# The diagonal mask of attention scores moved from TensorE to VectorE, and the reciprocals of the row sums from VectorE to GpSimd

## The reference, cut to what matters

```python
dots = jnp.einsum('bhid,bhjd->bhij', q, k) * jnp.exp(temperature)
eye = jnp.eye(n, dtype=bool)
dots = jnp.where(eye, NEG_MAX, dots)
attn = jax.nn.softmax(dots, axis=-1)
out = jnp.einsum('bhij,bhjd->bhid', attn, v)
```

## Time and profile before

| | before |
|---|---|
| median of 3 runs | 501.92 us (501.88 to 503.92) |
| profiled execution | 501.19 us |
| its span, first to last instruction | 499.4 us |
| TensorE clock granted, mean | 0.999 of full speed |
| busy: TensorE matmul | 478.2 us, 96% |
| busy: VectorE | 398.6 us, 80% |
| busy: ScalarE | 363.9 us, 73% |
| busy: GpSimd | 231.1 us, 46% |

### The profile page before, as it was taken

The page is one execution under the profiler, slowest core; times in us unless marked ns, Lnnn a source line. Parts: engine busy times, 40 slices in busy tenths (PEclk is TensorE's granted clock), DMA queues, the critical chain, the costliest instruction groups (busy, mean ns, idle before and its releaser), DMA issues.

```text
span 499.4 us, 11296 instructions
## 1 busy us (share of the span) xinstructions
PE 478.2 (96%) x3936; PEld 398.5 (80%) x3936; DVE 398.6 (80%) x738; ACT 363.9 (73%) x688; POOL 231.1 (46%) x226
## 2 busy tenths in 40 slices
PE   2999999999999999999999999999999999999887
PEld 2955788888888888888788888888888888888775
DVE  5469999878887887788887888788878899989455
ACT  1258788888788778877888688878887788683543
POOL 1112586667346734663246735663566345541000
PEclk9999999999999999999999999999999999999999
DMA  6500019432943295361612592349234933000002
GB/s 234 211 1 0 2 44 214 92 86 58 195 95 84 48 194 108 85 137 43 127 62 66 109 194 52 81 99 197 53 84 90 194 66 84 1 1 3 3 13 76
DMA packets 29483, 44.78 MB, mean 90 GB/s; under 512 B 3200, under 2 KB 21120, under 8 KB 29184
## 3 DMA queue, kind: packets, MB, share of 16 engines
q1 hardware_dynamic: 28864, 44.21, 37.6%
q10 hardware_dynamic: 576, 0.00, 0.1%
HBM read 6.46 MB, written 1.05 MB: 15 GB/s over the span
## 4 chain that ended last, share of the span: by engine, by line
PE 90%; DVE 5%; DMA 2%; ACT 2%; issue 1%; SPq 0%; POOL 0%; DVEq 0%; ACTq 0%
PE ps L686 24%; PE ps L670 22%; PE ps L654 11%; PE ps L655 11%; PE ps L596 5%; PE ps L729 3%; PE ps L591 2%; PE ps L658 2%; DMA arena<-in_wqkv_rows 2%; PE ps L877 2%; PE ps L860 2%; PE ps L891 1%; DVE pt_lo L1351 1%; DVE neg_max L1363 1%; PE ps L566 1%; PE ps L842 1%
## 5 line engine op out<-in xcount | busy, mean ns | idle before, releaser
L431 POOL TENSOR_SCALAR probs<-probs,inv_sum 128x1024 f32<-128x1024 f32 x128 | 144.8, 1131 | 184.3 <-DVE inv_sum L1357 181.6
L1363 DVE TENSOR_REDUCE neg_max<-ps 128x1 f32<-128x1024 f32 x128 | 156.6, 1223 | 63.9 <-PE ps L658 63.8
L1026 ACT ACTIVATE pt_hi<-ps 128x512 fp32r<-128x512 f32 x256 | 139.2, 595 | 39.7 <-PE ps L670 39.6
L1351 DVE TENSOR_TENSOR pt_lo<-ps,pt_hi 128x512 fp32r<-128x512 f32 x256 | 162.3, 676 | 1.5 <-ACT pt_hi L1026 1.5
L686 PE MATMUL ps<-pt_hi,v_slot 128*128 128x256 f32 x512 | 150.2, 326 | 0.0
L1046 ACT ACTIVATE probs<-ps,neg_max 128x1024 f32<-128x1024 f32 x128 | 142.5, 1113 | 1.5 <-DVE neg_max L1363 0.7
L670 PE MATMUL ps<-ident,probs 128*128 128x128 f32 x1024 | 133.8, 274 | 0.7 <-DVE v_all L1271 0.6
L686 PE MATMUL ps<-pt_lo,v_slot 128*128 128x256 f32 x512 | 127.7, 281 | 0.0
L670 PEld LDWEIGHTS ps<-ident,probs 128*128 128x128 f32 x1024 | 110.1, 141 | 1.3 <-DVE v_all L1271 0.7
L686 PEld LDWEIGHTS ps<-pt_hi,v_slot 128*128 128x128 f32 x512 | 96.6, 189 | 9.7 <-issue 9.7
L686 PEld LDWEIGHTS ps<-pt_lo,v_slot 128*128 128x128 f32 x512 | 96.8, 189 | 8.8 <-issue 8.8
(11 more groups left out here) (141 smaller groups left out, 404.8 us busy)
## 6 DMA issues: line engine op xcount, KB each, us to landing
q_st<-arena SPq DMA_DIRECT2D x28, 256.0 KB, 3.7
k_hi<-arena SPq DMA_DIRECT2D x28, 256.0 KB, 5.1
k_lo<-arena SPq DMA_DIRECT2D x28, 256.0 KB, 5.3
v_slot<-v_all SPq DMA_DIRECT2D x14, 512.0 KB, 3.9
arena<-arena SPq DMA_DIRECT2D x28, 256.0 KB, 5.4
f_sb<-in_f SPq DMA_DIRECT2D x2, 1024.0 KB, 10.7
x<-in_tok SPq DMA_DIRECT2D x2, 512.0 KB, 7.8
w_slot<-in_w_pairs SPq DMA_DIRECT2D x8, 128.0 KB, 2.1
```

The lines of the kernel that those rows point to most:

```text
L431: pool.tensor_scalar(probs[:, t % 4, :], probs[:, t % 4, :], inv_sum[:, t % 4:t % 4 + 1], 1.0, ALU.mult, ALU.mult).then_inc(norm_done, 1)
L1026: act.activation(dst, ps[:, transposes_bank(t, a, drain), :].rearrange("p (j c) -> p j c", c=P), ACT.Copy).then_inc(hi_done, 1)
L1351: dve.tensor_tensor(pt_lo[at], ps[:, transposes_bank(t, a, drain), :].rearrange("p (j c) -> p j c", c=P), pt_hi[at].bitcast(F32), ALU.subt ...
L1363: dve.tensor_reduce(neg_max[:, t % 4:t % 4 + 1], ps[:, SCORES + 2 * (t % 2):SCORES + 2 * (t % 2) + 2, :].rearrange("p a c -> p (a c)"), AX ...
```

## The change: what it does

In all head pairs but the first, TensorE's list loses the mask matmul, and the last score matmul counts `scores_ready`. VectorE gets a new function, `mask`: it waits for the scores, adds `neg_block` (a 128x128 f32 tile with -3e38 on its diagonal) in place to the diagonal block in PSUM, and counts `masked`. The maximum then waits for `masked`. In the first pair the mask stays on TensorE.

In all pairs the reciprocal leaves VectorE. GpSimd waits for the exponential (`exp_done`), raises the row sum to the power -1 into `inv_sum`, counts `recip_done`, waits for that, and normalises as before. Set-up on GpSimd gets three more instructions, so `N_CONST` goes from 12 to 15.

```diff
         def wait_apart(engine, semaphore, value):
...
+            const(pool.memset(neg_block[:, :], 0.0))
...
+            const(pool.memset(powers[:, 3 * NT:3 * NT + 1], -1.0))
...
-            for m, fill in ((ident, 1.0), (ident_b, 1.0), (neg_diag, NEG)):
+            for m, fill in ((ident, 1.0), (ident_b, 1.0), (neg_diag, NEG), (neg_block, NEG)):
...
                     for t in range(SPH):
                         split_qk(pair, k, t)
+                        wait_apart(pool, exp_done, pair.step0 + k * SPH + t + 1)
+                        pool.tensor_tensor(inv_sum[:, t % 4:t % 4 + 1], row_sum[:, t % 4:t % 4 + 1],
+                                           powers[:, 3 * NT:3 * NT + 1], ALU.pow).then_inc(recip_done, 1)
                         wait_apart(pool, recip_done, pair.step0 + k * SPH + t + 1)
...
                 own = t // 4
+                by_pe = pair.i == 0
                 for c in (1 - own, own):
...
-                    pe.matmul(bank, q, k_lo[:, k, half], start=False, stop=c != own)
-
-                bank = ps[:, SCORES + 2 * (t % 2) + own, :]
-                pe.matmul(bank[:, (t % 4) * P:(t % 4 + 1) * P], neg_diag[:, :], ident_b[:, :],
-                          start=False, stop=True).then_inc(scores_ready, 1)
+                    ins = pe.matmul(bank, q, k_lo[:, k, half], start=False, stop=c != own or not by_pe)
+
+                if by_pe:
+                    bank = ps[:, SCORES + 2 * (t % 2) + own, :]
+                    ins = pe.matmul(bank[:, (t % 4) * P:(t % 4 + 1) * P], neg_diag[:, :], ident_b[:, :],
+                                    start=False, stop=True)
+                ins.then_inc(scores_ready, 1)
...
-            def reciprocals(pair, k, t):
+            def mask(pair, k, t):
+
                 n = pair.step0 + k * SPH + t
-                dve.wait_ge(exp_done, n)
-                dve.reciprocal(inv_sum[:, (t - 1) % 4:(t - 1) % 4 + 1],
-                               row_sum[:, (t - 1) % 4:(t - 1) % 4 + 1]).then_inc(recip_done, 1)
+                dve.wait_ge(scores_ready, n + 1)
+                own = ps[:, SCORES + 2 * (t % 2) + t // 4, t % 4 * P:(t % 4 + 1) * P]
+                dve.tensor_tensor(own, own, neg_block[:, :], ALU.add).then_inc(masked, 1)
 
             def maxima(pair, k, t):
                 n = pair.step0 + k * SPH + t
-                dve.wait_ge(scores_ready, n + 1)
+                if pair.i == 0:
+                    dve.wait_ge(scores_ready, n + 1)
+                else:
+                    dve.wait_ge(masked, n + 1 - 2 * SPH)
...
+                        if pair.i > 0:
+                            mask(pair, k, t)
                         maxima(pair, k, t)
-                        if not (pair.i == 0 and k == 0 and t == 0):
-                            reciprocals(pair, k, t)
                         lagging(pair, k, t)
```

More of the change, by code:

```diff
@@ L73, in layer_kernel @@
         neg_diag = sb("neg_diag", [P, P], BF16)
+        neg_block = sb("neg_block", [P, P])
         ones = sb("ones", [P, P])
@@ L76, in layer_kernel @@
         tie = sb("tie", [P, GROUP])
-        powers = sb("powers", [P, 3 * NT])
+        powers = sb("powers", [P, 3 * NT + 1])
         emb_sb = sb("emb_sb", [P, D])
@@ L195, in layer_kernel @@
         scores_ready = sem("scores_ready")
+        masked = sem("masked")
         max_done = sem("max_done")
@@ L229, in layer_kernel @@
         stored = sem("stored")
-        N_CONST = 12
+        N_CONST = 15
         def wait_apart(engine, semaphore, value):
@@ L1389, in _ @@
             drain = Pair(8)
-            reciprocals(drain, 0, 0)
             for t in range(T_LAG):
```

## The result

The changed kernel takes 495.18 us (median of four runs, 494.73 to 495.47), against 501.9: a ratio of 0.9866, 95% interval 0.9847 to 0.9885. The forecast was 497.4 us, with a range of 494.3 to 502.0, so the kernel came out 2.2 us faster than forecast. The profiled execution took 495.01 us for a span of 493.2, so 6.2 us of span are to be explained (499.4 before).

What follows compares the result with a forecast made beforehand. TensorE was taken to bound the kernel, except where VectorE takes over in the last pair. Gains of 6.6 and 0.2 less 2.3 make 4.5 us: 501.19 to 496.7, plus 0.73 for the median, 497.4 us; range 494.3 to 502.0.

Steps and rivals of the forecast that it cites:

- TensorE's gap: Steps without TensorE's mask matmul: 0.065 us returned each, 6.6 us over 101 steps.
- The rival that TensorE returns nothing: Transposes' weights come late, so the gain is zero and the last pair loses about 2: 503.9 us, chance 0.10.
- The mask's price: VectorE's added in-place mask in PSUM with the maximum's wait on it: 0.33 us a step.
- M: Time on VectorE from the mask's start to the maximum's, taken as 0.33 us.
- The rival of a dear write to PSUM: VectorE's mask costs 0.42 to 0.49 us; at 0.46 the time is 500.1 us; chance 0.13.
- the threshold: In the middle pairs, VectorE's step exceeds TensorE's 2.755 us once the mask with its hop passes 0.435 us.
- The last pair: VectorE, also normalising there, is nearly full; eleven steps go from 34.33 to 36.6 us, 2.3 us lost.
- the last pair hides its part: Last pair's normalisations fall beside less GpSimd work, up to 2.3 us comes back: 495.1 us, chance 0.15.
- TensorE's saving is worth nothing there: Last pair's eleven steps: TensorE's own list is only 32.5 us, so shortening it gains nothing.
- Pair 0: First head pair: VectorE loses only 0.07 us a step, worth 0.2 us gained.
- GpSimd, I charge nothing: GpSimd's added powers, 0.74 us each in the first pair's busy middle, just fit before the transposes: cost zero.
- the 4.5 us of the sum: Whole kernel: 6.6 us gained, 0.2 gained in the first pair, 2.3 lost in the last.

Runs made afterwards that it cites:

- recip_only: The changed kernel, but TensorE masks in all pairs; GpSimd keeps the reciprocals. 501.97 us, ratio 1.0007.
- no_mask: The changed kernel with the diagonal mask of pairs 1 to 7 left out altogether. 493.87 us, ratio 0.9856.
- mask_only: The changed kernel with the reciprocals back on VectorE; the mask stays on VectorE. 496.31 us, ratio 0.9911.
- the wide masks: The changed kernel with VectorE's mask widened by zeros to 256 or 512 columns. 497.9 us (ratio 0.9911) and 515.86 us (1.0271).
- best_pad_18: The kernel best with 18 one-element float32 matmuls added near TensorE's start. 494.72 us, ratio 0.9846.
- before_pad_48: The kernel before the change with 48 one-element matmuls added near TensorE's start. 504.31 us, ratio 1.0042.
- mask_1_to_6: The changed kernel, but TensorE masks in pair 7 too, as in pair 0. 494.31 us, ratio 0.9838.
- best: The changed kernel, but TensorE also masks in steps 2 to 13 of pair 7, and VectorE takes pair 0's reciprocals. 493.96 us, ratio 0.9836.

## Why the prediction was right, and where its terms were off

**TensorE's gap: right.** Forecast 0.065 us a step between 0 and 0.07, measured 6.68 / 96 = 0.070. recip_only (310.69) and no_mask (303.99) show that the gain is the matmul gone from TensorE; mask_only shows that 0.95 of it would be lost again without GpSimd's part, whose worth there the prediction had at nothing. The Trainium skill's page "TensorE: Matmul & The Clock Gate", section "Back-to-back issue gap", has 56 and 81 ns for such a matmul; the measured 70 lies between, as the earlier trace rows did. The rival that TensorE returns nothing fell with the transposes' start at 128.06.

**The mask's price: right.** M is 0.34. The rival of a dear write to PSUM is refuted by the mask's row, and the threshold is borne out by the wide masks. The Trainium skill's page "VectorE: DVE Perf Modes", section on the TRN2 errata, gave an estimated 0.26 us. The measurement decides: the row is 0.30, and by width 0.30, 0.43 and 0.69 us for 128, 256 and 512 columns, about 1.02 ns a column and 0.17 us of start.

**The last pair: right in mechanism, its term too large.** I forecast 2.3 us lost for the eleven steps from maximum to maximum. They took 35.91 us (397.32 to 433.23) in place of 34.33, 1.58 lost; from scores to scores 1.35. The two maxima, and then the group of the normalised tiles between the eleven steps' scores (count, busy us, mean ns, idle before) before and after:

```profile
397.32 1.23 DVE L1377 TENSOR_REDUCE neg_max<-ps 128x1 f32<-128x1024 f32 x1
...
433.23 1.22 DVE L1377 TENSOR_REDUCE neg_max<-ps 128x1 f32<-128x1024 f32 x1
```

```profile
L1188 DVE TENSOR_SCALAR x<-h_sb,mv,rstd 128x128 f32<-128x128 f32 x6 | 3.3, 587 | 0.0
```

```profile
L1198 DVE TENSOR_SCALAR x<-h_sb,mv,rstd 128x128 f32<-128x128 f32 x6 | 2.7, 490 | 0.0
```

The main term that I had not counted is these normalisations: they became cheaper, their mean fell from 587 to 490 ns, 0.6 us for the six of eight in that stretch. In mask_only, where GpSimd's list is the old one, the mean is 590. That is a part of the rival "the last pair hides its part", and it came by GpSimd's new order, for which I had charged nothing either way. VectorE's rows from maximum to maximum, each counted from its start to the next one's, bear it out: the masks add 3.54 us, the reciprocals take 0.77 out and the idle time 0.31, much as in my sum, and the eight normalised tiles go from 3.66 to 2.96. Between recip_only and after, which differ by the mask alone, the eleven steps' scores show 1.8 (33.86 and 35.67): of the masks' 11 x 0.33 = 3.63 us, 1.1 fill VectorE's idle time ahead of the maxima, which is larger there than before (0.7), and 0.74 is an addition that falls behind the start of step 125's scores. My sentence that TensorE's saving is worth nothing there was too strong: where VectorE has no mask it is worth 0.66 (no_mask against recip_only), and in the changed kernel three of the eleven steps are 0.06 or 0.07 shorter than before.

**Pair 0: the step "GpSimd, I charge nothing" failed.** GpSimd's normalisations did end before their transposes, as I had worked out: the transposes that came late waited for VectorE. What I had not priced is what GpSimd's list does to VectorE: the normalisation beside it took 1.42 us in place of 0.59. Forecast 0.2 gained, measured 0.48 lost. The steps gain 0.29, near the 0.2, and step 13 loses 0.77; mask_only and best_pad_18, without GpSimd's powers there, get the loss back. The Trainium skill's page "SBUF — State Buffer", section "SBUF: two separate sides", says that VectorE (in a two-port mode, or with two inputs in SBUF beside a GpSimd operation that reads SBUF) and GpSimd share one pair of ports as an exclusive lock: whichever starts first has it for its whole instruction, and the other waits. For GpSimd's divisions, additions and splits the rows agree: the first tile begins at 75.09, 0.03 after GpSimd's division, and ends at 76.27, 0.08 after the division's end at 76.19. All tiles of before, after, mask_only, recip_only and no_mask that take more than 0.4 us end 0.08 to 0.09 us after such a GpSimd operation. For GpSimd's powers of one and four columns they don't agree: beside one of 1.0 us (454.75 to 455.79 in after) VectorE's tiles stay at 0.34, and there the measurement decides. Read ahead, that section would have put the third normalisation on the list of what GpSimd's new order can hit.

**The tail: not foreseen.** 1.22 us came from the place of TensorE's program, as the two kernels that only move it show (1.18 and 1.17 us); no step of the prediction looked at it, so this part of the gain is luck. The gap could have been read from the kernel before, as an idle stretch whose releaser is "issue"; that it would move with the length of the program could not be read from that one trace.

Term by term against the 4.5 us of the sum: the middle's six pairs 0.44 more than 96 x 0.065, the tail 1.22 more, the eleven steps 0.95 less lost, the last pair's other steps 0.2 less gained, pair 0 0.7 worse. Together 1.7 us, the distance from 496.7 to the 495.01 of the profiled execution. Without the tail it would be 0.5: the errors in the last pair and in pair 0, of opposite sign, nearly cancel.

**Open.** The gap that moves stands 199 or 200 records over a multiple of 256 in all eleven kernels that have it (all but before_pad_48), though at six different places of the program, and ends 1.2 to 1.6 us after a 16 KB transfer on the instruction queue has landed (before: begun at 478.50, landed at 479.42, gap to 480.70). That TensorE waits for its instructions there is read from this agreement and from the two kernels that only move the program; no row names the wait. What starts such a transfer, and so how long a gap will be for a given program, the runs don't show; my forecasts of where it stands, and of a program without it, failed.

## What to carry to other kernels

Moving a small operation from the engine that sets the step to one with room pays only where the room exists: read it stage by stage, add the hop from start to start and not the busy time, and leave the operation where it was in stages in which the other engine is full (here mask_1_to_6 and best). When a third engine gets new work, look for what it runs beside as well as for its own deadline. And before a difference of about 1 us in an untouched stage is explained by the change, look for idle time marked "issue" in both traces and ask whether the program merely moved.

## What the runs showed of the hardware

- VectorE's normalisation of one 128x128 tile in SBUF takes 0.33 us. A tile that begins while GpSimd divides, adds or splits in SBUF lasts until at least 0.08 us after GpSimd's operation has ended (up to 1.33 us in all); beside GpSimd's powers of one and four columns it keeps its time. VectorE's PSUM work (maximum 1.20 to 1.23 us, subtractions 0.66 to 0.69 each) kept its time in all twelve kernels.
- The instruction queue moves 16 KB at a time, 25 to 27 times in a run. In the tail's stretches of short matmuls TensorE stood for 0.16 to 1.69 us, once in each of eleven kernels, always 199 or 200 records over a multiple of 256. (A second such stretch, 0.26 us, stands 3.4 us before the end in all twelve; it keeps its place in the program and changes nothing.)
- A float32 matmul of one element counts as two weight loads and two matmuls in the profile, as one of 128 columns does (24 weight loads and 24 matmuls for the twelve of L573 in the changed kernel).
